# Grouped-query scalings as products on GpSimd, and turned probabilities copied first in a slot

## The reference

```
Q = (x @ Wq) -> 16 heads of 64;  K, V = x @ Wk, x @ Wv -> 4 heads of 64;  rope on Q and K
scores = Q K^T / 8 + polarity_bias + (1 - exp(-gamma * distance) * causal) * -1e9
attn   = softmax(scores);   out = (attn V) @ Wo
```

## Time and profile before

| | |
|---|---|
| median of 3 runs | 4328.75 us (4321.15 to 4343.08) |
| the profiled execution | 4331.27 us, span 4329.4 us |
| TensorE busy | 3895.7 us, 90% |
| VectorE, ScalarE, GpSimd busy | 3007.5 (69%), 2581.9 (60%), 2412.5 us (56%) |
| mean granted TensorE clock | 0.974 |

### The profile page before, as it was taken

One profiled execution on the slowest core, in us unless ns is written; L12 is line 12 of the kernel. 1 busy time (PEld: TensorE's weight loads), 2 busy tenths in 40 slices (PEclk: granted clock), 3 DMA queues, 4 the chain that ended last, 5 costly groups with the idle time before them and its releaser, 6 DMA issues. The chain is left out here.

```text
span 4329.4 us, 105712 instructions
## 1 busy us (share of the span) xinstructions
PE 3895.7 (90%) x37596; PEld 2560.4 (59%) x37596; DVE 3007.5 (69%) x8821; ACT 2581.9 (60%) x6209; POOL 2412.5 (56%) x3854
## 2 busy tenths in 40 slices
PE   3999999999999999999999999739599999999998
PEld 1565656556656556656565566526366666666666
DVE  4676776776777767767767676561577778778786
ACT  2656556556566566565565565402377777777776
POOL 3656557566576575565665664525455545555552
PEclk7999999999999999999999999959799999999999
DMA  4323334334243243343342432223422424334231
GB/s 128 72 77 86 80 76 94 74 89 94 59 104 79 70 91 77 75 89 79 84 94 66 97 83 66 69 75 61 66 53 48 69 46 59 61 48 68 46 56 26
DMA packets 168566, 317.06 MB, mean 73 GB/s; under 512 B 21680, under 2 KB 112112, under 8 KB 162928
## 3 DMA queue, kind: packets, MB, share of 16 engines
q1 hardware_dynamic: 162928, 300.88, 32.6%
q0 software_dynamic: 3968, 5.25, 0.7%
q10 hardware_dynamic: 1152, 4.19, 0.3%
HBM read 126.66 MB, written 32.59 MB: 37 GB/s over the span
## 5 line engine op out<-in xcount | busy, mean ns | idle before, releaser
L1420 POOL TENSOR_SCALAR l_prob_wo<-l_prob_wo,l_recip_g 128x384 f32<-128x384 f32 (+3 forms) x768 | 926.8, 1217 | 265.5 <-DVE l_recip_g L980 261.5
L1871 DVE TENSOR_REDUCE l_neg_max<-l_bank 128x1 f32<-128x512 f32 x1024 | 680.2, 684 | 260.6 <-PE l_bank L1710 258.9
L1997 ACT ACTIVATE l_pts<-l_bank 128x512 f32<-128x512 f32 x1024 | 593.0, 596 | 297.3 <-PE l_bank L1725 288.4
L1248 ACT ACTIVATE l_prob_wo<-l_prob_wo,l_neg_max_g 128x128 f32<-128x128 f32 (+3 forms) x1024 | 571.2, 559 | 299.1 <-DVE l_neg_max_g L974 293.2
L961 DVE CUSTOM_DVE_ANT_0 l_bank<-l_bank,l_mask 128x128 f32<-128x128 f32 (+3 forms) x1024 | 500.7, 500 | 318.0 <-PE l_bank L648 309.7
L1240 ACT ACTIVATE l_pts<-l_bank 128x128 f32<-128x128 f32 (+3 forms) x1024 | 437.3, 436 | 424.3 <-PE l_bank L666 407.7
L974 DVE CUSTOM_DVE_ANT_0 l_prob_wo<-l_bank,l_bias 128x128 f32<-128x128 f32 (+3 forms) x1024 | 475.9, 483 | 285.8 <-PE l_bank L699 263.3
L710 PE MATMUL l_bank<-ident,l_prob_wo 128*128 128x128 f32 x2560 | 428.4, 284 | 83.6 <-POOL l_prob_wo L1420 40.5
L710 PEld LDWEIGHTS l_bank<-ident,l_prob_wo 128*128 128x128 f32 x2560 | 291.0, 141 | 318.0 <-issue 180.1
L1710 PE MATMUL l_bank<-next_ks,l_qs 96*128 96x512 bf16 x1024 | 393.5, 385 | 46.6 <-DVE l_neg_max L1871 23.2
L1725 PEld LDWEIGHTS l_bank<-l_qs,next_ks 128*128 128x128 bf16 x4096 | 303.5, 97 | 181.3 <-ACT l_pts L1997 30.6
(11 more groups left out here) (262 smaller groups left out, 8042.7 us busy)
## 6 DMA issues: line engine op xcount, KB each, us to landing
l_bias<-bias SPq DMA_DIRECT2D x128, 512.0 KB, 4.4
l_qs<-l_parts SPq DMA_DIRECT2D x192, 128.0 KB
l_qs<-l_qs SPq DMA_DIRECT2D x96, 256.0 KB
l_x<-in_x SPq DMA_DIRECT2D x32, 512.0 KB, 5.0
l_kT<-l_bias SPq DMA_DIRECT2D x128, 128.0 KB, 3.2
l_qT<-l_arena SPq DMA_DIRECT2D x128, 128.0 KB, 3.0
l_qT<-l_bias SPq DMA_DIRECT2D x128, 128.0 KB, 3.0
l_prob_wo<-in_Wo SPq DMA_DIRECT2D x16, 1024.0 KB, 4.7
```

The lines of the kernel that those rows point to most:

```text
L1248: nc.scalar.activation(prob[qt][:, i, :], prob[qt][:, i, :], ACT.Exp, bias=neg_max_g[:, k:k + 1], scale=-1.0, accum_out=sums_g[:, k:k + 1] ...
L1420: nc.gpsimd.tensor_scalar(prob[qt][:, i, :], prob[qt][:, i, :], recip_g[:, k:k + 1], None, ALU.mult).then_inc(s.g_scaled, 1)
L1871: nc.vector.tensor_reduce(neg_max[:, n % (2 * UNITS):n % (2 * UNITS) + 1], S[n % SB][:, :], AX.X, ALU.max, negate=True).then_inc(s.max_rea ...
L1997: nc.scalar.activation(pts[:, q % 2, u % H, :, :], TB[u % 2][:, :].rearrange("p (j q) -> p j q", j=NT), ACT.Exp, scale=DS ** -0.5).then_in ...
```

## The change

All 1024 scalings of the grouped-query attention go to GpSimd; VectorE had 256 of them. The operation becomes a product of two tensors, the second one the reciprocal broadcast along the row, in place of a multiplication by a pointer scalar. TensorE's transposes then wait for one semaphore, `g_scaled`, that counts in program order. On VectorE the copy of the transposed block comes ahead of the slot's maximum and reciprocal, on ScalarE ahead of the slot's exponential; in the first slots of the next frame it comes ahead of the last reciprocal on VectorE.

```diff
-        def scaled_on_pool(p, i):
-            return i == 0 or p % NT > 1
-
-        def scaled(b, p, i):
...
@@ turn_g (TensorE)
-                    pe.wait_ge(*scaled(b, p, i))
+                    pe.wait_ge(s.g_scaled, UNITS * b + 2 * p + i + 1)
@@ reciprocal_g (VectorE)
-                    if not scaled_on_pool(p, 1):
-                        dve.wait_ge(s.g_recip, BEATS * b + p + 1)
-                        v = prob[p % NT][:, 1, :]
-                        nc.vector.tensor_scalar(v, v, recip_g[:, k + 1:k + 2], None, ALU.mult).then_inc(s.g_scaled_v, 1)
@@ VectorE's slots
+                        if r >= 71 and r % 2:
+                            copy_g(f, (r - 71) // 2)
                         if r >= 64:
                             biased_max(f, (r - 64) // 2, r % 2)
                         if r >= 67 and r % 2:
                             reciprocal_g(f, (r - 67) // 2)
-                        if r >= 71 and r % 2:
-                            copy_g(f, (r - 71) // 2)
                     if there(f - 1):
+                        if r in (1, 3, 5):
+                            copy_g(f - 1, 29 + (r - 1) // 2)
                         if r == 1:
                             reciprocal_g(f - 1, 31)
-                        if r in (1, 3, 5):
-                            copy_g(f - 1, 29 + (r - 1) // 2)
@@ ScalarE's slots
+                        if r >= 72 and r % 2 == 0:
+                            copy_g(f, (r - 72) // 2)
                         if r >= 65:
                             exponentials_g(f, (r - 65) // 2, (r - 65) % 2)
-                        if r >= 72 and r % 2 == 0:
-                            copy_g(f, (r - 72) // 2)
@@ scale (GpSimd)
-                    nc.gpsimd.tensor_scalar(prob[qt][:, i, :], prob[qt][:, i, :], recip_g[:, k:k + 1], None, ALU.mult).then_inc(s.g_scaled, 1)
+                    v = prob[qt][:, i, :]
+                    nc.gpsimd.tensor_tensor(v, v, recip_g[:, k:k + 1].to_broadcast([P, (qt + 1) * P]), ALU.mult).then_inc(s.g_scaled, 1)
@@ GpSimd's slots
                         if r >= 68:
-                            if scaled_on_pool((r - 68) // 2, r % 2):
-                                scale(f, (r - 68) // 2, r % 2)
+                            scale(f, (r - 68) // 2, r % 2)
```

More of the change, by code:

```diff
@@ L544, in layer0 @@
             sem(n) for n in ("scores_ready", "max_ready", "split", "max_turned", "max_placed", "t_ready", "exp_ready", "pv_ready", "out_turned"))
-        s.g_scores, s.g_max, s.g_exp, s.g_recip, s.g_scaled, s.g_scaled_v, s.g_turned, s.g_copied_v, s.g_copied_a, s.g_pv, s.g_out = (
-            sem("g_" + n) for n in ("scores", "max", "exp", "recip", "scaled", "scaled_v", "turned", "copied_v", "copied_a", "pv", "out"))
+        s.g_scores, s.g_max, s.g_exp, s.g_recip, s.g_scaled, s.g_turned, s.g_copied_v, s.g_copied_a, s.g_pv, s.g_out = (
+            sem("g_" + n) for n in ("scores", "max", "exp", "recip", "scaled", "turned", "copied_v", "copied_a", "pv", "out"))
         s.w_ready = sem("w_ready")
```

## The result

The changed kernel takes 4354.27 us, median of ten runs (4347.54 to 4363.57), against 4333.24 for the kernel before, timed in turn with it: a ratio of 1.0049 [1.0038, 1.006]. That is 21 us more: slower by an amount that the interval keeps clear of zero, within the predicted range, and at the edge of the 0.5% that the prediction calls no change. The forecast had +7.5 us.

The account below looks back on a forecast made before the run. TensorE was taken to bound the kernel, with 82.7 us (1.9%) about the ceiling of any gain. Terms of -0.25 us a frame over 15 frames (-3.8) and +0.8 in 14 (+11.2) gave +7.5 us: 4336 us, range 4296 to 4372.

Parts of the forecast that it names:

- What bounds the kernel: TensorE sets the time, at full granted clock; its 82.7 us idle ahead of the transposes is about the gain's ceiling.
- The scalings: GpSimd's products take 0.31, 0.62, 0.95, 1.27 us by width, nothing fixed on top; 6.3 us a group instead of 7.3.
- Group 0 to 1: Reciprocal 2.1 us late behind VectorE's copy, so transposes of pair 0.3 wait 0.8 us; net +0.25 us a frame.
- the walk: The prediction's tracing of one first-layer frame's engine timelines, group by group: -0.25 us a frame, +0.8 in 14 frames.
- Group 2 to 3, 6 and 7: TensorE's waits on GpSimd's scalings and on copies there: -0.3, -0.3 and +0.1 us a frame respectively.
- Group 5 to 6, the largest term: Slot 115's copy and later x load delay the maximum TensorE waits on: +0.8 us in 14 frames, 11.2 together.
- What would show it: Signs: products' times, L710's idle some 60 us, L699's 35 or more, slot 115's wait 2.1, frame 168.4 plus 0.5.
- Faster: Rival: new stalls find cover and only the gains stay, 2 us a frame, -32 in all: 4297 us; chance 0.20.
- Slower by stalls: Rival: maxima behind copies delay scores 0.3 us in all eight groups of each frame, 38 us: 4367; chance 0.17.
- Slower by price: Rival: a product on GpSimd costs what a pointer scaling cost, 36 us more: 4372 us; chance 0.12.
- Two inputs twice one: Rival: GpSimd's products cost twice the scalings, some 1070 us more: 5400 us; chance 0.01.

## Why the prediction was right, point by point

The forecast's size held by luck, through errors that offset each other: the gains were larger than counted, and one loss, priced at the length of its wait, cost several times that.

*What bounds the kernel.* TensorE, as said. But "at the full granted clock" was read from one undisturbed half frame and carried over to all frames after the change. The trace of before already had 10.2 us at half clock, after its longer stalls at slot 115 (1.67, 2.32 and 2.38 us, not after the eleven others, 1.31 to 1.63). This is the step that failed: after the change the half clock came to 88.7 us and TensorE's busy time to 32.0 us more, a term that the sum does not have.

*The scalings.* 256 wide was right (0.63 against 0.62). The others were off: 0.41 for 0.31, 0.83 for 0.95, 1.05 for 1.27. The four rows lie 0.20 to 0.22 apart, on some 0.2 us that all have in common, so "nothing fixed on top" was wrong; the 1.27 was the row of another form, two full tensors. A group of pairs costs 2 x (0.41 + 0.63 + 0.83 + 1.05) = 5.8 us, not 6.3. The two products that set group 0's chain are the cheaper ones.

*Group 0 to 1.* The reciprocal is late by just the 2.1 us worked out, the last product is not. VectorE's copy, the maximum and the reciprocal, then GpSimd's products, then TensorE, four timelines' rows beside the earlier trace rows; 6.49 us are to be taken off:

```profile
1027.45 0.29 DVE L980 COPY l_pts<-l_bank 128x128 f32<-128x128 f32 x1 [3.59 <-PE l_bank L671]
1027.66 0.68 DVE L965 CUSTOM_DVE_ANT_0 l_prob_wo<-l_bank,l_bias 128x512 f32<-128x512 f32 x1
...
1028.26 0.16 DVE L971 RECIPROCAL l_recip_g<-l_sums_g 128x2 f32<-128x2 f32 x1
```

```profile
1028.50 1.61 POOL L1408 TENSOR_TENSOR l_prob_wo<-l_prob_wo,l_recip_g 128x384 f32<-128x384 f32 x2 [3.97 <-DVE l_recip_g L971]
...
1033.29 1.06 POOL L1408 TENSOR_TENSOR l_prob_wo<-l_prob_wo,l_recip_g 128x512 f32<-128x512 f32 x1
```

```profile
1033.99 1.09 PE L701 MATMUL l_bank<-ident,l_prob_wo 128*128 128x128 f32 x8
...
1035.52 0.63 PE L701 MATMUL l_bank<-ident,l_prob_wo 128*128 128x128 f32 x2 [0.44 <-DVE l_pts L980]
```

1028.26 - 6.49 = 21.77 where the walk had 21.78. But the last product ends at 1034.35, just ahead of the second half of the eight transposes, which did not wait; the wait of 0.8 is not there, and the waits at the start of group 1 came down from 0.62 + 0.27 to 0.44 + 0.03: -0.42 in place of +0.25.

*Group 2 to 3, 6 and 7.* The 0.68 went, scores 3.1 wait 0.33 instead of the 0.6 expected: -0.37 for -0.3. Group 6's 1.10 became 0.85: -0.25 for -0.3. Group 7's 0.86 became 0.44, with 0.16 more and 0.22 less at two later turns, and a new wait of 0.52 (below): +0.04 for +0.1. These held.

*Group 5 to 6, the largest term.* The stall grew from 1.57 us to 2.41 in the mean of the 14 frames: +0.84 for the +0.8 worked out. The copy's 0.47 is as read. The other part was mis-sized: against TensorE's own progress x is asked for 0.57 us later and not 0.3, and the loads land 0.18 us faster in the mean, so that the sum's agreement is partly luck. The price was wrong. At 14 x 0.84 = 11.8 us the stall would have left the change a gain. But the old order at group 5 alone, which takes 12.2 us off the stall, gives back 46 us by the ratios, and asking for x earlier, which takes off all 33.8, gives back 70.

*What would show it.* L710's idle was to fall to 60 and fell to 47.6; L699's was to rise to 35 or more and rose to 45.7; the wait ahead of 6.3 was to be 2.1 and is 2.36; undisturbed frames, predicted at 168.9, are 168.1 to 169.2 (168.2 to 169.0 before). The sum of the idle time thus came out on the gain's side: 35.1 less, 21.0 more, and 7.2 more ahead of the small scores of L639. The walk missed these last: 14 waits of 0.52 us at the start of the next frame's scores. The trace names no releaser, but the kernel lets these scores wait for the batch's last maximum, and in slot 127 the copy of pair 7.0 now stands ahead of it (VectorE, then TensorE):

```profile
1104.85 0.28 DVE L980 COPY l_pts<-l_bank 128x128 f32<-128x128 f32 x1
1105.05 0.68 DVE L965 CUSTOM_DVE_ANT_0 l_prob_wo<-l_bank,l_bias 128x512 f32<-128x512 f32 x1
```

```profile
1105.83 0.22 PE L639 MATMUL l_bank<-l_ks,l_qs 96*128 96x128 bf16 x1 [0.52 <-issue]
```

With the 32.0 us of busy time the sum is +25, close to the span's +24.0. Of the prediction's own signs of being wrong two came true: the product of 512 is at 1.05 and not at 1.27, and maxima also hold scores 6.1, which the walk did not have.

*The rivals.* "Faster" had its gain nearly right: its -32 us stand beside the products' -39, measured alone, but the order's stalls found no cover. "Slower by stalls", a delay in all eight groups, is not what happened: L690's new waits stand ahead of 6.3 (33.8 us), 3.1 (5.3) and 6.1 (4.0) and hardly elsewhere. "Slower by price" and "Two inputs twice one" fell with the products' row. No rival had the clock in it.

## What to carry to other kernels

A wait of the bounding engine is not to be priced by its length alone: look in the trace for what the granted clock did after the longest waits that are already there, since a slightly longer one can bring the same on many more frames. When an instruction that waits for another engine is moved ahead in an in-order queue, list everything behind it, loads that another queue issues upon it too, and follow the chain once around all engines; VectorE's new order, which with its partner on ScalarE was at 0.9887, was at 1.0251 where ScalarE kept the old one. And try the parts of a bundled change alone: here one part was worth 0.9% and the others took back more than that.

## What the runs showed of the hardware that was not expected

The granted clock of a kernel whose TensorE is over 90% busy still fell to half after single stalls of 1.7 to 2.7 us, for 3.4 to 13.7 us. It did not fall after each: in the changed kernel 2.47 us left it alone and 2.29 did not, and with the one copy moved in the kernel before it fell after 10 of 14 stalls of 1.69 to 1.94 us. Nor does it take one long stall: with VectorE's new order alone 33 of the 34 falls stand at a pair of waits of 0.44 and 1.38 us, as in the rows of that run. The Trainium skill, "TensorE: Matmul & The Clock Gate", Part 1, has the clock follow how busy the array has lately been, and gives it an idle and a busy level; the rows agree on two levels (0.50 and 1.00, the others being stretches that hold both). Which of the stalls is followed by a fall was not settled here.

On GpSimd the price went by the form of the operands: at 512 f32, a product with a broadcast second operand took 1.05 us, a sum or difference of two full tensors 1.28, a scaling by a pointer scalar 1.57, a multiplication and addition by constants 0.63. Chance collisions with other engines don't make the difference: the 256 scalings of this width took 1.55 to 1.66 us, the 256 products 1.03 to 1.14.
